# The context of an attention is turned by VectorE in 32x32 squares instead of by TensorE

## The reference

```python
# 1: cross attention of the normalised x with the context
h = layernorm(x) @ hW.T + hb;  c = ctx @ cW.T + cb
q = h @ qW.T + qb;  k = c @ kW.T + kb;  v = c @ vW.T + vb
attn = softmax(q @ k.T / sqrt(512))          # 512 x 8192 per batch
x = x + (attn @ v + q) @ oW.T + ob
# 2: a state space layer: input projection, long convolution, gate
xn = norm(layernorm(x)) * ln_g + ln_b
u, z = split(xn @ in_w.T + in_b)
y = long_convolution(u, kernel(A_log, B, C, log_dt)) * silu(z)
x = x + clip(y @ out_w.T + out_b + residual, -10, 10)
# 3: each row goes to the one of 8 experts with the largest gate logit
x = x + expert_w[argmax(layernorm(x) @ gate_w + gate_b)] ...
```

## Time and profile before

| | us |
|---|---|
| runs of the kernel, median of 3 (lowest to highest) | 1283.92 (1283.85 to 1284.06) |
| profiled execution, its own time | 1280.48 |
| profiled execution, span | 1278.8 |
| attention of batch 0, about | 147 to 558 |
| between the batches, about | 558 to 626 |
| attention of batch 1, about | 626 to 1037 |

### The profile page before, as it was taken

The page is one execution under the profiler, slowest core; times in us unless marked ns, Lnnn a source line. Parts: engine busy times, 40 slices in busy tenths (PEclk is TensorE's granted clock), DMA queues, the critical chain, the costliest instruction groups (busy, mean ns, idle before and its releaser), DMA issues.

```text
span 1278.8 us, 17356 instructions
## 1 busy us (share of the span) xinstructions
PE 1203.6 (94%) x5953; PEld 985.3 (77%) x5953; DVE 910.0 (71%) x1847; ACT 493.8 (39%) x1091; POOL 327.9 (26%) x312
## 2 busy tenths in 40 slices
PE   7999999999999999999999999999999999926397
PEld 6787788888888888888788888888888888825275
DVE  7853577777777777775277777777777766797584
ACT  4211244444444444442433333333333352322252
POOL 4613122222111111212122222222222231824234
PEclk9999999999999999999999999999999999968699
DMA  7311010001000100120011011000100010104692
GB/s 259 108 34 33 1 67 34 34 33 66 33 33 33 66 33 33 34 108 1 3 65 34 34 37 61 33 33 35 64 33 33 34 66 34 67 1 173 208 352 105
DMA packets 29054, 81.25 MB, mean 64 GB/s; under 512 B 4383, under 2 KB 4415, under 8 KB 24912
## 3 DMA queue, kind: packets, MB, share of 16 engines
q1 hardware_dynamic: 25648, 70.69, 15.6%
q0 software_dynamic: 3360, 9.97, 2.2%
HBM read 74.35 MB, written 8.13 MB: 65 GB/s over the span
## 4 chain that ended last, share of the span: by engine, by line
PE 85%; DVE 9%; DMA 2%; POOL 1%; ACT 1%; issue 1%; SPq 0%; POOLq 0%; DVEq 0%; ACTq 0%
PE bank L456 38%; PE bank L607 28%; PE bank L464 5%; PE bank L594 4%; PE bank L819 2%; PE bank L691 2%; PE bank L660 2%; DMA zT<-in_L_ffn_expert_w_dram 1%; DVE probs L1301 1%; DMA spectra<-mixed,gather_rows 1%; POOL rows L1797 1%; DMA stage<-in_L_xattn_hW_dram 1%; PE bank L490 1%; DVE bnst L1157 1%; DVE h L1301 0%
## 5 line engine op out<-in xcount | busy, mean ns | idle before, releaser
L938 ACT ACTIVATE probs<-bank,nbias 128x512 f32<-128x512 f32 x128 | 88.1, 688 | 448.7 <-DVE nbias L1364 448.7
L1371 DVE TENSOR_TENSOR probsT<-bank,probsT 128x512 fp32r<-128x512 f32 x128 | 88.5, 692 | 176.3 <-ACT probsT L930 176.2
L607 PE MATMUL bank<-hl_A,probsT 128*128 128x512 f32 x768 | 195.1, 403 | 1.8 <-POOL hl_A L1679 1.8
L607 PE MATMUL bank<-hl_F,probsT 128*128 128x512 f32 x768 | 195.2, 403 | 1.2 <-POOL hl_F L1679 1.2
L456 PE MATMUL bank<-hl_B,hl_D 128*128 128x512 f32 x768 | 192.3, 399 | 0.0
L456 PE MATMUL bank<-hl_C,hl_D 128*128 128x512 f32 x768 | 191.5, 398 | 0.0
L607 PEld LDWEIGHTS bank<-hl_A,probsT 128*128 128x128 f32 x768 | 139.8, 189 | 30.9 <-issue 2.0
L607 PEld LDWEIGHTS bank<-hl_F,probsT 128*128 128x128 f32 x768 | 139.8, 189 | 30.2 <-issue 1.4
L1679 POOL TENSOR_TENSOR hl_F<-stage,hl_F 128x512 fp32r<-128x512 f32 x62 | 80.0, 1291 | 321.2 <-ACT hl_F L921 321.2
L456 PEld LDWEIGHTS bank<-hl_C,hl_D 128*128 128x128 f32 x768 | 140.2, 188 | 27.5
L1679 POOL TENSOR_TENSOR hl_A<-stage,hl_A 128x512 fp32r<-128x512 f32 x62 | 80.1, 1292 | 314.2 <-ACT hl_A L921 314.2
(11 more groups left out here) (386 smaller groups left out, 1750.3 us busy)
## 6 DMA issues: line engine op xcount, KB each, us to landing
stage<-in_ctx_dram SPq DMA_DIRECT2D x32, 1024.0 KB, 4.8
stage<-in_L_ffn_expert_w_dram SPq DMA_DIRECT2D x9, 1024.0 KB, 8.1
stage<-in_L_attn_in_w_dram SPq DMA_DIRECT2D x4, 1024.0 KB, 5.9
zT<-in_L_ffn_expert_w_dram SPq DMA_DIRECT2D x3, 1024.0 KB, 7.6
rows<-in_L_ffn_expert_w_dram SPq DMA_DIRECT2D x3, 1024.0 KB, 6.2
xb<-in_x_dram SPq DMA_DIRECT2D x2, 1024.0 KB, 13.3
spectra<-in_L_attn_in_w_dram SPq DMA_DIRECT2D x2, 1024.0 KB, 5.4
mixed<-xb SPq DMA_DIRECT2D x2, 1024.0 KB, 4.6
```

What stands on the lines that cost most here:

```text
L607: last = nc.tensor.matmul(obank[u % 2][:], probsT[u % 2][:, a, j, :], nat[b][par][:, c, j, :], start=(j == 0 and (a, c) == PASSES[0]), sto ...
L938: nc.scalar.activation(probs[u % 2][:], sbank[u % 2][:], ACT.Exp, bias=nbias[:, q:q + 1], scale=SCALE, accum_out=rsum[:, q:q + 1]).then_in ...
L1371: nc.vector.tensor_tensor(probsT[u % 2][:, 1], tbank[u % 2][:].rearrange("p (j q) -> p j q", j=T), probsT[u % 2][:, 0].bitcast(F32), ALU.s ...
```

## The change

TensorE's context transposes go. SyncE loads every chunk a second time, by `load_squares`: four transfers, one for each 128 features (`j`), that lay the context out so that the 32 partitions of group j hold rows (mod 32) and the free dimension holds 16 groups of 32 rows by 128 features. VectorE's 32x32 transposes then give the features on the partitions, in an order of features that `q_to_ctx` is brought to as well (`in_squares_order`). VectorE turns a block in place, one step ahead of its use (`next_square`); ScalarE makes the high part from it and GpSimd the low part, which VectorE had made. The squares lie in `yT` and `uT` in batch 0 and in `xb` in batch 1, so x is stored in DRAM (`put_x`) and loaded back (`x_back`). The first chunks are turned by VectorE too (`first_square`, `first_chunk`, `first_lo`), that of batch 1 in the last four steps of batch 0. The rows of a chunk are now taken as `(j p)` instead of `(p j)`.

```diff
-        sbank, tbank, obank, cbank = bank[0:2], bank[2:4], bank[4:6], bank[6:8]
+        sbank, tbank, obank = bank[0:2], bank[2:4], bank[4:6]
+        square_rows = [[m.rearrange("p t n -> p (t n)").rearrange("p (i w) -> p i w", w=P) for m in pair] for pair in (
+            (yT, uT), (xb[:, 1], xb[:, 0]))]
+        squares = [[m.rearrange("p i (m c) -> p m i c", c=SQUARE) for m in pair] for pair in square_rows]
...
+            return w.rearrange("p (m i c) -> p m i c", m=T, c=SQUARE)      (by_squares)
-        ctx_rows = ctx_in.rearrange("b (c p j) d -> (b c) p j d", p=P, j=T)
+        ctx_rows = ctx_in.rearrange("b (c j p) d -> (b c) p j d", p=P, j=T)
+        ctx_squares = ctx_in.rearrange("b (c i a) (j w) -> (b c) j a i w", c=NCH, a=SQUARE, j=T)
...  SyncE
                 for c in range(2, NCH):
                     if c > 2:
-                        sp.wait_ge(cT_ready, blocks + T * (c - 2))
+                        sp.wait_ge(cT_split, blocks + T * (c - 2))
+                        load_squares(b, c)
                     sp.wait_ge(nat_split, base + T * (c - 1))
                     load(f"chunk{c}@{b}", ctx_rows[b * NCH + c])
+                    if b == 0 and c == 3:
+                        put_x(1)
+                    if b == 0 and c == 5:
+                        sp.wait_ge(x_put[1], 16)
+                        load_squares(1, 0)
...
+            def load_squares(b, c):
+                for j in range(T):
+                    sp.dma_start(square_rows[b][c % 2][SQUARE * j:SQUARE * (j + 1)], ctx_squares[b * NCH + c, j]
+                                 ).then_inc(in_squares[b][c % 2], 16)
...
             load("chunk0@0", ctx_rows[0])
+            sp.wait_ge(inbias_ready, 1)
+            for c in range(2):
+                load_squares(0, c)
+            sp.wait_ge(c0_split, T)
+            load_squares(0, 2)
             attention_loads(0)
...  TensorE
-                pe.wait_ge(in_stage[0], LANDED["chunk0@0"])
-                transposes("ctx0T.#@0", stage[0])
...
-                    turned(cbank[dd % 2], stage[par], dd).then_inc(cT_ready, 1)
...
-                        if not (last and u >= T):
-                            context_block(t, u)
...
-                pe.wait_ge(in_stage[0], LANDED["chunk0@1"])
-                transposes("ctx0T.#@1", stage[0])
...  ScalarE
-                    nc.scalar.activation(ctxT[par][:, 0, dd, :], cbank[dd % 2][:], ACT.Copy).then_inc(cT_hi, 1)
+                    if dd == 0:
+                        wait_pos(act, scores_ready, base, t * UN + u)
+                    nc.scalar.activation(by_squares(ctxT[par][:, 0]...)[:, dd], squares[b][par][:, dd], ACT.Copy
+                                         ).then_inc(cT_hi, 1)
...
-                round_jobs("q_to_ctx.#", hlB)
+                round_in_squares_order("q_to_ctx.#", hlB)
...  VectorE
+            def first_square(b, k):
+                if k == 0:
+                    dve.wait_ge(in_squares[b][0], 16 * T)
+                nc.vector.transpose(squares[b][0][:, k], squares[b][0][:, k]).then_inc(c0_ready, 1)
...
-                def context_block(t, u):
-                    par, dd = (u // T + 1) % 2, u % T
-                    dve.wait_ge(cT_hi, t * UN + (blocks + u + 1))
-                    nc.vector.tensor_tensor(ctxT[par][:, 1, dd, :], cbank[dd % 2][:], ctxT[par][:, 0, dd, :].bitcast(F32),
-                                            ALU.subtract).then_inc(cT_split, 1)
+                def next_square(t, u):
+                    par, dd = ((u + 1) // T + 1) % 2, (u + 1) % T
+                    if dd == 0:
+                        dve.wait_ge(in_squares[b][par], t * (16 * T) + 2 * (16 * T))
+                    nc.vector.transpose(squares[b][par][:, dd], squares[b][par][:, dd]).then_inc(cT_ready, 1)
...
-                        if not (last and u >= T):
-                            context_block(t, u)
+                        if not (last and u + 1 >= T):
+                            next_square(t, u)
+                        if last and u >= T and b == 0:
+                            first_square(1, u - T)
                         maxima(t, u)
...  GpSimd
+                def context_block(t, u):
+                    par, dd = (u // T + 1) % 2, u % T
+                    pool.wait_ge(cT_hi, t * UN + (blocks + u + 1))
+                    nc.gpsimd.tensor_tensor(by_squares(ctxT[par][:, 1]...)[:, dd], squares[b][par][:, dd],
+                                            by_squares(ctxT[par][:, 0]...)[:, dd].bitcast(F32), ALU.subtract
+                                            ).then_inc(cT_split, 1)
                 def trip(t, first, last):
                     for u in range(UN):
+                        if not (last and u >= T):
+                            context_block(t, u)
                         if not (last and u + 2 >= UN):
                             natural(t, u)
```

More of the change, by code:

```diff
@@ L35 @@
 HALF = S // 2
+SQUARE = 32
 NBANK = 8
@@ L88 @@
 AFTER = [JOB[f"inT0.0@{b}"] for b in range(B)]
-AHEAD = JOB["ctx0T.0@1"]
-BANK = [(n - AFTER[int(n >= AFTER[1])] + 6 + (T if AHEAD <= n < AFTER[1] else 0)) % NBANK for n in range(len(JOBS))]
+BANK = [(n - AFTER[int(n >= AFTER[1])] + 6) % NBANK for n in range(len(JOBS))]
 BEFORE = [max((m for m in range(n) if BANK[m] == BANK[n]), default=None) for n in range(len(JOBS))]
@@ L272, in build @@
         cT_ready, cT_hi, cT_split = sem("cT_ready"), sem("cT_hi"), sem("cT_split")
+        c0_ready, c0_hi, c0_split = sem("c0_ready"), sem("c0_hi"), sem("c0_split")
+        in_squares = [[sem(f"in_squares{b}{n}") for n in range(2)] for b in range(B)]
+        x_put, x_back = ([sem(f"{n}{b}") for b in range(B)] for n in ("x_put", "x_back"))
         nat_hi, nat_split = sem("nat_hi"), sem("nat_split")
         pv_ready, sums_updated = sem("pv_ready"), sem("sums_updated")
+        x_kept = nc.dram_tensor("x_kept", [B, P, T * D], F32)
         mixed = nc.dram_tensor("mixed", [TOKENS, 2 * D], F32)
@@ L409, in _ @@
                 load(f"chunk{c}@1", ctx_rows[NCH + c])
+            put_x(0)
+            sp.wait_ge(x_put[0], 16)
+            load_squares(1, 1)
+            sp.wait_ge(c0_split, 2 * T)
+            load_squares(1, 2)
             sp.wait_ge(term_added, TERMS)
@@ L828, in _ @@
             middle()
-            attention(1, "U1i.1@0", [f"ctx0T.{T - 1}@1", "U1i.0@0"])
+            attention(1, "U1i.1@0", ["U1i.0@0"])
             tail()
@@ L841, in round_jobs, with round_in_squares_order, first_chunk @@
                     round_job(name.replace("#", str(k)), slot[:, 0, k, :])
+            def round_in_squares_order(name, slot):
+                for k in range(T):
+                    job = name.replace("#", str(k))
+                    act.wait_ge(filled, JOB[job] + 1)
+                    nc.scalar.activation(slot[:, 0, k, :].rearrange("p (m j c) -> p m j c", m=T, c=SQUARE),
+                                         in_squares_order(bank[BANK[JOB[job]]][:]), ACT.Copy).then_inc(rounded, 1)
+            def first_chunk(b):
+                if b == 1:
+                    filled_by(act, "u.3@0")
+                for k in range(T):
+                    act.wait_ge(c0_ready, T * b + k + 1)
+                    nc.scalar.activation(by_squares(ctxT[0][:, 0].rearrange("p m n -> p (m n)"))[:, k], squares[b][0][:, k], ACT.Copy
+                                         ).then_inc(c0_hi, 1)
             def round_rows(name, slot):
@@ L1217, in prepare @@
                 last.then_inc(kbias_ready, 1)
-                lo_jobs("q_to_ctx.#", hlB)
+                lo_in_squares_order("q_to_ctx.#", hlB)
                 keep_and_split("q1", lambda k: queries(1, k), qT[1], hlF)
@@ L1251, in prepare @@
                     add_to_x(f"qo0.{k}", 0, k)
-                lo_jobs("ctx0T.#@0", ctxT[0])
+                for k in range(T):
+                    first_square(0, k)
+                first_lo(0)
                 filled_by(dve, "ubias")
@@ L1415, in trip @@
                             sums(*((t, u - 2) if u >= 2 else (t - 1, u - 2 + UN)))
+                dve.wait_ge(in_squares[b][1], 16 * T)
+                nc.vector.transpose(squares[b][1][:, 0], squares[b][1][:, 0]).then_inc(cT_ready, 1)
                 dve.wait_ge(sums_zeroed, 3 * (b + 1) + 1)
@@ L1673, in attention @@
             def attention(b):
-                base = b * STEPS
+                base, blocks = b * STEPS, b * BLOCKS
                 def natural(t, u):
```

54 lines of the change are left out of this document (40 added, 14 removed).

## The result

| | before | after |
|---|---|---|
| median | 1283.99 us (1283.85 to 1284.64, 4 runs) | 1364.88 us (1363.94 to 1367.28, 4 runs) |
| profiled execution, its own time | 1280.48 us (span 1278.8) | 1367.28 us (span 1365.5) |

The ratio is 1.0632, 95% interval 1.0613 to 1.065: the change costs 80.9 us. The forecast was 1381, so +97.

What follows compares the result with a forecast made beforehand. VectorE's loop and TensorE were both taken to bound batch 0 at about 6.44 us a step, TensorE batch 1; 66.6 + 32.0 + 2.2 - 3.8 = +97.0 us gave 1381 us, range 1335 to 1468 (81%).

Steps and rivals of the forecast that it cites:

- Two engines at their limit: Batch 0's attention step before the change: VectorE's loop runs at its own 6.439 us, TensorE's at 6.437.
- The hold-up: Attention steps: GpSimd's new low part makes a VectorE instruction wait, 1.11 us each time, from 1.05 to 1.30.
- the rule of two inputs: A VectorE instruction with two SBUF inputs stands still until a running GpSimd instruction has ended; PSUM readers are not held.
- First element, forecast 66.6 + 2.2: Batch 0: 60 steps held 1.11 us each, +66.6; turning batch 1's first chunk in the last four steps, +2.2.
- Second element, forecast +32.0: Batch 1: 38 steps with products at 7.70 us and 22 without at 5.71, against 60 at 6.437: +32.0 us.
- The transposes: pitch 0.62 us, forecast 0.60: VectorE's 120 transposes replace 120 PSUM subtractions at the same pitch of 0.60 us, so this term is 0.
- The rival of a dear transpose: VectorE's transpose takes up to 1.30 us, adding +87 us, total 1468; chance 12%.
- Chunk transposes, forecast -3.8: TensorE loses two chunks of four blocks outside the loops, 1.9 us each, in TensorE-bound stretches: 3.8 us gained.
- Loads in the attention: Each chunk's second read, four transfers of 256 KB, is hidden, asked for about 19 us ahead: 0 us.
- Nobody is held up: Rival: GpSimd's low part delays no VectorE instruction in the attention steps, -11.8 us, total 1272; chance 12%.
- TensorE's clock: Rival: the clock falls because TensorE idles 1.7 us per 7.55 us step; slower than 1381, 4% together with late loads.
- TensorE 5.88 us a step: Attention step without context transposes: TensorE needs 5.88 us, from 6.44 less 0.56 of transposes.

Runs made afterwards that it cites:

- experiment 7: The kernel before, with GpSimd's natural copy made to wait for VectorE's running sum of the step before: 1283.35 us, ratio 1.0006.
- experiment 1: The changed kernel, with GpSimd's low part made to wait for VectorE's running sum of the same step: 1264.22 us, ratio to before 0.9872.
- experiment 6: The changed kernel, with only GpSimd's natural copy made to wait for VectorE's running sum of the step before: 1221.88 us, ratio to before 0.9524.
- number 1: Same run as experiment 1: the changed kernel with GpSimd's low part waiting for the step's running sum, 1264.22 us.
- experiment 5: The changed kernel, with GpSimd's natural copy waiting for the previous step's running sum and its low part for the step's row maximum: 1229.75 us, ratio to before 0.9597.
- experiment 4: The changed kernel, with VectorE's running sum moved behind the row update and transpose, GpSimd untouched: 1306.39 us, ratio to before 1.0174.

## Why the prediction was right

**Two engines at their limit: shown.** Freeing VectorE alone gives 0 us (experiment 7). Freeing TensorE alone, with VectorE's loop as long as it was (experiment 1), leaves the first element at 6.43 us a step; the 16 us that it gains over the kernel before lie mostly in the second (388.2 us in place of 399.1), where VectorE's loop had been the shorter one all along (steps of 6.6 and 5.7 us against TensorE's 6.44). Both together give 61 us.

**The hold-up: right in place and mechanism, a little too dear.** I took 1.11 us. Measured are 7.47 - 6.44 = 1.03 us in the first element, which is `lsum`'s 1.24 - 0.21, and 7.67 - 6.58 = 1.09 for the second product. The lower bound I had, `lsum`'s 1.05 in the earlier trace rows, was the nearer one, since the held instruction in the first element is `lsum` itself. The order that I had argued from the tail is the one in the step: `natural`, term, low part, `lsum`. There was a little luck in the argument: the held instructions of the earlier trace rows have one SBUF input, so they showed the taking of turns, but not by the rule of two inputs that I had put ahead of them.

**First element, forecast 66.6 + 2.2, measured +58.5.** 60 x (1.11 - 1.03) is 4.8 of the difference. I had also charged all 60 steps; 56 intervals show the long step, and 4 x 1.03 is 4.1. The first `nbias` interval was 4.39 us before and 2.42 after, so the entry into the loop gained 2 us that I had not counted. The last five intervals take 31.6 us in place of 29.1, the +2.2 that I had charged (2.5).

**Second element, forecast +32.0, measured +27.0.** The two step lengths were forecast at 7.70 and 5.71 and measured at 7.67 and 5.70. The count was off: I took 60 such steps, 38 of them long, and the trace has 55, 35 of them long, which took 29.0 us more than before. That is 3.0 of the 5. The first three intervals together take 15.3 us in both kernels. The last five, all but the first without a context block and put at nothing by me, take 27.8 us in place of 29.9: the other 2.1.

**The transposes: pitch 0.62 us, forecast 0.60.** The rival of a dear transpose is out. Of the two pages of the Trainium skill set against each other in the prediction, the trace agrees with the Vector Engine (DVE) Microarchitecture Reference ("The reshape front-end and per-opcode configuration"), which has one element per cycle and lane: the pitch of 0.62 us is close to the 0.60 of VectorE's other instructions on 512 elements. The estimate of 1.24 us from the Trainium skill's VectorE: DVE Perf Modes ("The three transpose paths") was twice the measured pitch; the page's figure is for bf16 and a single 128x128, and four of them don't add up to one instruction of 512.

**Chunk transposes, forecast -3.8.** The stretch between the elements fell by 2.2 us, where 1.9 was forecast. The other 1.9, ahead of the first element, did not come in this execution: the first scores' weight load starts at 147.50 us in place of 147.25. VectorE waited 4.95 us for the first squares to land, and they and their low part came within 0.4 us of holding TensorE up. Whether the 1.9 us are there is not settled: the first `nbias` starts at 151.4 and 150.7 us in the two executions without the change (before and experiment 7), and anywhere from 148.7 to 151.9 in the seven with it.

**Loads in the attention: 0, shown.** No wait for the squares appears in the attention, the transfers of 256 KB land in 5.1 us, and experiment 6 does all the loads and is the fastest.

**What the rivals were worth.** "Nobody is held up" had 12% at 1272; the experiment that makes it true by placement, number 1, measured 1264. TensorE's clock, of which I feared a loss, did fall: 15 times to 0.50 for some 3 us in the attentions, 0.96 in a 40 us window, against 1.00 before. The steps in which it fell are no longer than their neighbours (7.42 to 7.48 us in the first element, 5.67 in the second), since VectorE sets the pace and TensorE has idle time to lose. In the attentions it costs nothing that shows; in the tail it has part in the 3 us.

**One number of the prediction's first part is wrong.** I gave TensorE 5.88 us a step without the context transposes, by taking off the 0.56 us of their weight loads. Placed, the step is 5.98 us with TensorE never idle. What the transposes took from the step is 0.46 us. The trace of before has this number as well, in the last steps of an element, which have no context block (scores, TensorE's matmuls, start to start 5.98 us):

```profile
529.15 2.91 PE L456 MATMUL bank<-hl_C,hl_D 128*128 128x512 f32 x12
...
535.13 2.91 PE L456 MATMUL bank<-hl_C,hl_D 128*128 128x512 f32 x12
```

In the same steps `nbias` follows `nbias` at 5.86 us, which I took for TensorE's pace in the expectation of experiment 5. It is VectorE's, whose loop is without its subtraction of 0.60 us there; in experiment 7 these steps take 5.98. The forecast hardly hung on the number (the +2.2 is made from it), but experiment 5's did, and most of what experiments 6 and 7 show follows from it: 120 x 0.46 = 55 of the 61 us.

## What to carry to other kernels

Before giving work to an idle GpSimd, write down what VectorE executes at the moment when it will run: if that instruction has two inputs in SBUF, it will stand still until GpSimd's has ended, even if it has one element per partition. An instruction with one SBUF input is not safe for that alone; look for its duration beside a running GpSimd instruction. The remedy costs one wait: make GpSimd's instruction wait for the VectorE instruction behind which only such follow as run undisturbed beside it, here `rows`, the transpose and the maxima.

When two engines are at their limit together, a fix for one shows little by itself. Here relieving VectorE gave 0 us, relieving TensorE 16, and both 61; try them together before giving one up.

A busy share does not tell work from standing still. VectorE's busy time rose by 101 us with 8 instructions more; the mean duration of an instruction of one element per partition (0.86 us against 0.21) was the row that showed it. TensorE's stayed the same with 512 instructions fewer; there it was the pitch of its matmuls and the granted clock of a 2 us window.

## What was unexpected of the hardware

- The two engines take turns by whole instructions even where VectorE's follow each other within 0.1 us. Cutting GpSimd's instruction in two let VectorE's next one in between (`lsum` 1.24 to 0.69 us), though GpSimd's work became longer in sum (1.87 us for the two, waits included, against 1.74).
- The transpose of 32x32 squares, in fp32 and in place, 128 x 512 elements: 0.70 us, pitch 0.62, and it neither holds a GpSimd subtraction up nor is held up by it (1.29 us beside it, experiment 1).
- TensorE's granted clock fell to 0.50 for 2.1 to 3.4 us at a time, 15 times in the attentions of the changed kernel, where TensorE is idle for some 0.8 us in a step of the first element, and never in those of before and of experiments 6 and 7, where it is not idle. A window of 40 us shows it as 0.96. No step was longer for it.
- A `scalar_tensor_tensor` with one input in SBUF and one in PSUM (`rows`) isn't held up (0.73 us beside the low part, experiment 4); the same operation with both in SBUF (`zT`) is (1.77 to 1.81 us against 0.74).
